# A mixture-of-experts kernel on one core: the first two tiles of each expert taken as a pair, with the weights held still and the tokens streamed

## The reference, cut to what matters

```python
xn = layernorm(x)                       # x: 2 x 1024 x 512, fp32; T = 2048 tokens
# routing: each token picks 6 of 32 experts
s = sigmoid(xf @ Wr.T + br)             # ... group-limited top-6 -> idx, weights w
gate = zeros(T, 32).at[arange(T)[:, None], idx].add(w)
# experts: W1 is 32 x 256 x 512, W2 is 32 x 512 x 256
for w1, w2, g in experts:
    acc += g[:, None] * (square(relu(xf @ w1.T)) @ w2.T)
shared = square(relu(xn @ Ws1.T)) @ Ws2.T
out = x + causal_attention(xn) + shared + acc
```

## Time and the profile before

| | |
|---|---|
| median of 3 runs | 1529.18 us (1529.16 to 1531.23) |
| the profiled execution, its own time | 1530.99 us |
| its span, first to last instruction | 1529.2 us |
| PE busy | 1516.1 us, 99% of the span |
| DVE busy | 1133.2 us, 74% |
| ACT busy | 838.2 us, 55% |
| POOL busy | 296.5 us, 19% |

### The profile page before, as it was taken

One profiled execution on the slowest core, in us unless ns is written; L12 is line 12 of the kernel. 1 busy time (PEld: TensorE's weight loads), 2 busy tenths in 40 slices (PEclk: granted clock), 3 DMA queues, 4 the chain that ended last, 5 costly groups with the idle time before them and its releaser, 6 DMA issues.

```text
span 1529.2 us, 31143 instructions
## 1 busy us (share of the span) xinstructions
PE 1516.1 (99%) x8548; PEld 1308.5 (86%) x8549; DVE 1133.2 (74%) x2586; ACT 838.2 (55%) x1753; POOL 296.5 (19%) x540
## 2 busy tenths in 40 slices
PE   9999999999999999999999999999999999999998
PEld 7887888989888978888888888888888888888886
DVE  7887566666666669949948958966975994994896
ACT  5565666766766635535535634544553563553553
POOL 0002443444444301012002002102102101200211
PEclk8999999999999999999999999999999999999999
DMA  7875677777776712102102103412211210210111
GB/s 277 322 283 188 199 240 235 242 236 226 237 257 200 240 41 70 43 21 75 42 20 75 42 34 103 164 62 82 68 35 36 74 41 21 75 34 27 56 42 55
DMA packets 64774, 184.34 MB, mean 121 GB/s; under 512 B 7136, under 2 KB 7264, under 8 KB 60000
## 3 DMA queue, kind: packets, MB, share of 16 engines
q1 hardware_dynamic: 39888, 112.56, 20.9%
q0 software_dynamic: 16640, 54.54, 13.0%
q10 hardware_dynamic: 8208, 16.78, 2.8%
HBM read 123.29 MB, written 60.56 MB: 120 GB/s over the span
## 4 chain that ended last, share of the span: by engine, by line
PE 97%; DVE 2%; DMA 1%; ACT 0%; issue 0%; SPq 0%; DVEq 0%; ACTq 0%
PE bank L663 8%; PE bank L665 8%; PE bank L994 8%; PE bank L664 8%; PE ps_s L663 7%; PE ps_s L665 7%; PE ps_s L664 7%; PE ps_s L981 5%; PE ps_s L983 4%; PE ps_s L982 4%; PE ps_s L861 4%; PE ps_s L865 3%; PE ps_s L884 3%; PE ps_s L862 3%; PE ps_s L885 3%; PE ps_s L888 3%
## 5 line engine op out<-in xcount | busy, mean ns | idle before, releaser
L1323 ACT ACTIVATE probs<-probs,negmax 128x128 f32<-128x128 f32 (+7 forms) x256 | 197.4, 773 | 122.6 <-DVE negmax L1737 121.9
L1331 ACT ACTIVATE pT_hi<-bank 128x512 fp32r<-128x512 f32 x288 | 164.4, 595 | 143.6 <-PE bank L994 117.6
L1348 DVE TENSOR_TENSOR pT_lo<-bank,pT_hi 128x512 fp32r<-128x512 f32 x288 | 189.6, 684 | 41.1 <-ACT pT_hi L1331 40.1
L1737 DVE CUSTOM_DVE_ANT_0 probs<-ps_s,causal 128x128 f32<-128x128 f32 (+7 forms) x256 | 189.3, 752 | 17.2 <-PE ps_s L983 15.7
L427 POOL TENSOR_TENSOR settled<-ident 128x1 f32<-128x1 f32 x192 | 46.0, 239 | 789.0 <-DVE acc L1766 779.0
L994 PE MATMUL bank<-ident,probs 128*128 128x128 f32 x1152 | 157.0, 272 | 0.0
L994 PEld LDWEIGHTS bank<-ident,probs 128*128 128x128 f32 x1152 | 136.9, 141 | 19.8
L663 PE MATMUL ps_s<-xT_hi,wa_hi 128*128 128x512 f32 x384 | 152.7, 398 | 0.0
L665 PE MATMUL ps_s<-xT_hi,wa_lo 128*128 128x512 f32 x384 | 151.0, 393 | 0.0
L664 PE MATMUL ps_s<-xT_lo,wa_hi 128*128 128x512 f32 x384 | 150.3, 391 | 0.0
L1746 DVE TENSOR_SCALAR probs<-probs,rnorm 128x128 f32<-128x128 f32 (+7 forms) x256 | 133.4, 521 | 9.1
(11 more groups left out here) (197 smaller groups left out, 3608.7 us busy)
## 6 DMA issues: line engine op xcount, KB each, us to landing
eraw<-we SPq DMA_DIRECT2D x37, 1024.0 KB, 7.4
expert_outputs<-ysb SPq DMA_DIRECT2D x111, 256.0 KB
araw<-wa SPq DMA_DIRECT2D x37, 512.0 KB, 3.8
expert_outputs<-comb ACTq DMA_DIRECT2D x1, 16384.0 KB, 44.2
normed_tokens<-xn SPq DMA_DIRECT2D x4, 1024.0 KB, 9.8
out<-acc SPq DMA_DIRECT2D x16, 256.0 KB, 2.6
acc<-x SPq DMA_DIRECT2D x2, 1024.0 KB, 13.7
turned_tokens<-xT_hi SPq DMA_DIRECT2D x2, 1024.0 KB, 6.3
```

The costliest lines, as they stand in the source:

```text
L1323: act.activation(pr, pr, ACT.Exp, bias=negmax[:, i % 2, a:a + 1], scale=-1.0, accum_out=rowsum[:, i % 2, a:a + 1]).then_inc(exp_ready, 1)
L1331: act.activation(pT_hi[:, blk % RING, :], ps_t[blk % 2][:, :], ACT.Copy).then_inc(pt_hi_ready, 1)
L1348: dve.tensor_tensor(out_, whole, upper.bitcast(F32), ALU.subtract).then_inc(signal, 1)
L1737: dve.tensor_tensor_reduce(halves(probs[:, i % 2, a, 0:keys]), ps_s[:, s:s + parts, 0:keys // parts], halves(causal[:, SQ - keys:]), -1.0, ...
```

## The change

The first two tiles of each expert become a pair. In their first layer the weights are stationary, 128 hidden units at a time, and the 256 tokens of both tiles stream past them (`hidden_pair`). The result comes out with hidden units on the partitions, so these two tiles need no `transpose_hidden`. The hidden values of the pair are made in two halves `m` on ACT and DVE. The output of the pair's first tile runs directly behind (`output_first`); that of the second is the `output_tile` of the next loop iteration. The remaining tiles run as before. Every expert is given at least three tiles (`LEAST`). The weight pieces 2 and 3 move from behind the tile loop into the pair.

```diff
-MAXT = MINT + 2 * E
+LEAST = 3
+MAXT = max(LEAST * (E - n) + min(n * TILES, (T * TOPK + (P - 1) * n) // P) for n in range(E + 1))
...
+        ps_x2 = banks[0][:, :]
+        ps_p = [bank[:, 0:2 * P] for bank in banks[1::2]]
+        ps_y2 = banks[2][:, :]
...
+            def hidden_pair(lo, s):
+                w_hi, w_lo = w1(hi_slot(s)), w1(lo_slot(s))
+                both = lambda x, k: x[:, k, :, :].rearrange("p t n -> p (t n)")
+                for m in range(KM):
+                    ms = slice(m * P, (m + 1) * P)
+                    if m == 0:
+                        pe.wait_ge(mx_hi, lo + 2)
+                    for k in range(KD):
+                        pe.matmul(ps_p[m], w_hi[:, k, ms], both(xgT_hi, k), start=(k == 0), stop=False)
+                        pe.matmul(ps_p[m], w_lo[:, k, ms], both(xgT_hi, k), start=False, stop=False)
+                    if m == 0:
+                        pe.wait_ge(mx_lo, lo + 2)
+                    for k in range(KD):
+                        mm = pe.matmul(ps_p[m], w_hi[:, k, ms], both(xgT_lo, k), start=False, stop=(k == KD - 1))
+                    mm.then_inc(mh_ready, 1)
+
+            def output_first(lo, s):
+                w_hi, w_lo = w2(hi_slot(s)), w2(lo_slot(s))
+                for m in range(KM):
+                    pe.wait_ge(mhhi_ready, past(lo + (m + 1)))
+                    pe.matmul(ps_y2, hT_hi[:, m, 0, :], w_hi[:, m, :], start=(m == 0), stop=False)
+                    pe.matmul(ps_y2, hT_hi[:, m, 0, :], w_lo[:, m, :], start=False, stop=False)
+                    pe.wait_ge(mhlo_ready, past(lo + (m + 1)))
+                    mm = pe.matmul(ps_y2, hT_lo[:, m, 0, :], w_hi[:, m, :], start=False, stop=(m == KM - 1))
+                mm.then_inc(my_ready, 1)
...
             def expert_tiles(e, s, lo, hi, es):
-                pe.wait_ge(ew_lo, (e + NSH) * WP + 2)
-                hidden_tile(lo, slot_of(s))
-                after = pair_bound(pe, e + 2)
+                turn_tokens(lo + 1, ps_x2)
                 if s:
                     output_tile(lo - 1, slot_of(s - 1))
                 else:
                     with pe.If(es > 0):
                         output_tile(lo - 1, slot_of(SLOTS - 1))
-                transpose_hidden(lo, (e + (NSH + 1)) * WP)
-                with pe.Fori(lo + 1, hi) as p:
+                after = pair_bound(pe, e + 2)
+                pe.wait_ge(ew_lo, (e + NSH) * WP + 2)
+                hidden_pair(lo, slot_of(s))
+                pe.sem_inc(mt_ready, 2)
+                turn_tokens(lo + 2, ps_x)
+                pe.wait_ge(ew_lo, (e + (NSH + 1)) * WP)
+                output_first(lo, slot_of(s))
+                with pe.Fori(lo + 2, hi) as p:
                     hidden_tile(p, slot_of(s))
                     output_tile(p - 1, slot_of(s))
                     transpose_hidden(p)
...
             def expert_uppers(e, s, lo, hi, es):
-                relu_hidden(lo)
-                upper_tokens(lo + 1)
+                upper_tokens(lo + 1, 1)
                 upper_weights(0, slot, arrived)
...
-                upper_hidden(lo)
                 after = pair_bound(act, e + 2)
                 upper_weights(1, slot, arrived)
-                with act.Fori(lo + 1, hi) as p:
+                relu_pair(lo, 0)
+                upper_pair(lo, 0)
+                upper_weights(2, slot, arrived)
+                relu_pair(lo, 1)
+                upper_pair(lo, 1)
+                upper_tokens(lo + 2)
+                copy_output(lo, ps_y2)
+                upper_weights(3, slot, arrived)
+                with act.Fori(lo + 2, hi) as p:
...
-                upper_weights(2, slot, arrived)
-                upper_weights(3, slot, arrived)
...
             def expert_lowers(e, s, lo, hi, es):
-                square_hidden(lo)
-                lower_tokens(lo + 1)
+                lower_tokens(lo + 1, 1)
                 lower_weights(e + 2, 0, slot)
-                lower_hidden(lo)
                 after = pair_bound(dve, e + 2)
                 lower_weights(e + 2, 1, slot)
-                with dve.Fori(lo + 1, hi) as p:
+                square_pair(lo, 0)
+                lower_pair(lo, 0)
+                lower_weights(e + 2, 2, slot)
+                square_pair(lo, 1)
+                lower_pair(lo, 1)
+                lower_tokens(lo + 2)
+                lower_weights(e + 2, 3, slot)
+                with dve.Fori(lo + 2, hi) as p:
...
-                chain(dve.tensor_scalar(pairs_f, pairs_f, 2.0, None, ALU.max))
+                chain(dve.tensor_scalar(pairs_f, pairs_f, float(LEAST), None, ALU.max))
...
+                        if isinstance(n, int) and n == 0 and unit == 0:
+                            dve.wait_ge(room_free, 1)
```

More of the change, by code:

```diff
@@ L219, in moe_attention_kernel @@
             xg = sb("xg", [P, XG, D], F32, room)
[L220 to L221 removed]
+            xgT_hi = sb("xgT_hi", [P, KD, 2, P], F32R, room)
+            xgT_lo = sb("xgT_lo", [P, KD, 2, P], F32R, room)
             ysb = sb("ysb", [P, YB, D], F32, room)
@@ L224, in moe_attention_kernel @@
             mhsq = sb("mhsq", [P, M], F32, room)
-            hT_hi = sb("hT_hi", [P, KM, P], F32R, room)
-            hT_lo = sb("hT_lo", [P, KM, P], F32R, room)
+            hT_hi = sb("hT_hi", [P, KM, 2, P], F32R, room)
+            hT_lo = sb("hT_lo", [P, KM, 2, P], F32R, room)
+            prelu = sb("prelu", [P, KM, 2 * P], F32, room)
+            phsq = sb("phsq", [P, KM, 2 * P], F32, room)
         with ExitStack() as room:
@@ L1242, in relu_hidden, with relu_pair, upper_pair, copy_output @@
                 act.activation(mrelu[:, :], ps_h, ACT.Relu).then_inc(mrelu_ready, 1)
+            def relu_pair(lo, m):
+                act.wait_ge(mh_ready, lo + (m + 1))
+                act.wait_ge(mhsq_ready, past(lo))
+                act.activation(prelu[:, m, :], ps_p[m], ACT.Relu).then_inc(mrelu_ready, 1)
+            def upper_pair(lo, m):
+                act.wait_ge(mrelu_ready, past(lo + (m + 1)))
+                act.activation(hT_hi[:, m, :, :].rearrange("p t n -> p (t n)"), prelu[:, m, :],
+                               ACT.Square).then_inc(mhhi_ready, 1)
             def upper_hidden(p):
                 act.wait_ge(mt_ready, p + 1)
-                act.activation(hT_hi[:, :, :], ps_g.rearrange("p (m n) -> p m n", m=KM), ACT.Copy).then_inc(mhhi_ready, 1)
-            def copy_output(p):
+                act.activation(hT_hi[:, :, 1, :], ps_g.rearrange("p (m n) -> p m n", m=KM), ACT.Copy).then_inc(mhhi_ready, 1)
+            def copy_output(p, bank=ps_y):
                 act.wait_ge(my_ready, past(p + 1))
                 act.wait_ge(y_free, p + 1)
-                act.activation(ysb[:, bass.ds(p % YB, 1), :].rearrange("p s d -> p (s d)"), ps_y,
+                act.activation(ysb[:, bass.ds(p % YB, 1), :].rearrange("p s d -> p (s d)"), bank,
                                ACT.Copy).then_inc(y_copied, 1)
@@ L1647, in _, with lower_tokens, square_pair, lower_pair @@
             dve.tensor_copy(tok_idx[:, 0:MAXT], ps_list).then_inc(list_ready, 1)
-            def lower_tokens(q):
+            def lower_tokens(q, second=0):
                 dve.wait_ge(mx_hi, q + 1)
-                subtract(xgT_lo[:, :, :], ps_x.rearrange("p (k n) -> p k n", k=KD), xgT_hi[:, :, :], mx_lo)
+                subtract(xgT_lo[:, :, second, :], (ps_x, ps_x2)[second].rearrange("p (k n) -> p k n", k=KD),
+                         xgT_hi[:, :, second, :], mx_lo)
+            def square_pair(lo, m):
+                dve.wait_ge(mrelu_ready, past(lo + (m + 1)))
+                dve.tensor_tensor(phsq[:, m, :], prelu[:, m, :], prelu[:, m, :], ALU.mult).then_inc(mhsq_ready, 1)
+            def lower_pair(lo, m):
+                dve.wait_ge(mhhi_ready, past(lo + (m + 1)))
+                dve.wait_ge(mhsq_ready, past(lo + (m + 1)))
+                subtract(hT_lo[:, m, :, :].rearrange("p t n -> p (t n)"), phsq[:, m, :],
+                         hT_hi[:, m, :, :].rearrange("p t n -> p (t n)"), mhlo_ready)
             def square_hidden(p):
@@ L1659, in lower_hidden @@
                 dve.wait_ge(mhhi_ready, past(p + 1))
-                subtract(hT_lo[:, :, :], ps_g.rearrange("p (m n) -> p m n", m=KM), hT_hi[:, :, :], mhlo_ready)
+                subtract(hT_lo[:, :, 1, :], ps_g.rearrange("p (m n) -> p m n", m=KM), hT_hi[:, :, 1, :], mhlo_ready)
             def lower_weights(e, c, slot):
```

50 lines of the change are left out of this document (24 added, 26 removed).

## The result

The changed kernel takes 1543.25 us (median of 4 runs, 1539.38 to 1546.65) against 1529.2: ratio 1.0102, 95% interval 1.0075 to 1.0129. It is slower by about 1%. The profiled execution's own time is 1546.65 us.

The account below looks back on a forecast made before the run. PE was taken to bound the kernel, so only its work and waits count. +0.41 us per expert times 31 gave +12.7, with +0.7 and +0.6 +14.0 us: 1545.0, less 1.8 for the median, 1543.2 us; range 1533 to 1554.

Parts of the forecast that it names:

- The sum: Per expert -0.43 - 0.20 + 0.71 + 0.33 = +0.41 us; times 31, +12.7; with +0.7 and +0.6, +14.0 us.
- The change of expert, +0.71: At the old expert's last output PE waits for ACT's `hT_hi`: latency 1.15 less 0.44 us cover, at 31 changes.
- Rival A: PE doesn't wait at the change of expert: 1521 us, or 1511 with no wait in the pair; chance 0.06.
- The pair, +0.33: In the pair, waits of 0.05 for `hT_hi` and 0.15 for `hT_lo`, plus 0.13 us loop entry, per expert.
- the entry of the tile loop: Behind the pair, entering the tile loop straight after a wait costs PE 0.13 us per expert.
- Rivals B and C: B: the pair costs PE nothing, 1533 us, chance 0.15. C: it costs twice as much, 1554 us, chance 0.12.
- The hidden transposes, -0.43: Four hidden transposes fewer on PE for each expert, 2 x 0.22 = 0.43 us saved.
- The old excess, -0.20: PE's old wait at the end of an expert's first tile, behind weight pieces 2 and 3, goes: 0.20 us per expert.
- Front and first expert, +0.7 and +0.6: Longer lists add 0.7 us to PE's mask products; in the first expert the third tile starts 0.6 us later.
- Rival D: Idle time at each change of expert lowers PE's clock: +53 us, 1597 us; chance 0.04.

Follow-up runs that it names:

- e2_fill: Changed kernel with three more 512-column products at each change of expert, between the next tokens' transposes and the last tile's output: 1552.71 us, ratio 1.0156.
- e6_merge: Changed kernel with the second tile's token transposes moved into the previous expert's last tile, under one branch tree with the first tile's: 1561.95 us, ratio 1.0210.
- e4_win: Changed kernel with the pair's first layer put ahead of the previous expert's last output and the second tile's tokens transposed earlier: 1520.16 us, ratio 0.9946.
- e5_win2: e4_win with the transposes of the next pair's two token tiles under one branch tree instead of two: 1509.59 us, ratio 0.9869.
- e11_behind: Kernel before with an added two-level branch tree on TensorE right behind each expert's first tile's hidden transposes: 1564.11 us, ratio 1.0211.
- e3_late2: Changed kernel with weight piece 2 moved from between the pair's halves to behind the split of the third tile's tokens: 1536.14 us, ratio 1.0045.
- e9_few: Kernel before with VectorE's subtraction of each expert's last weight piece cut to 8 columns: 1526.70 us, ratio 0.9974.
- e1_maxt: Kernel before with only its lists of tiles lengthened from 160 to 177, nothing of the pair: 1527.55 us, ratio 0.9984.
- e10_again: The changed kernel run once more, unchanged: 1543.38 us, ratio 1.0079.
- e7_soon: Kernel before with the third of four weight pieces put ahead of the loop over tiles instead of behind it: 1539.42 us, ratio 1.0078.

## Why the prediction was right

**The sum.** I forecast 1543.2 and measured 1543.25 and 1543.38. That is luck, closer than the terms: the experts cost 15.5 us instead of 13.3 (12.7 and the first expert's 0.6), and the attention stage gave back 2.6 that I didn't have. 15.5 - 2.6, with the 0.7 of the front, is 13.6. The mechanism is borne out all the same: per expert I had +0.41, and measured are 0.49 (15.5 less 0.3 for the first expert, over 31).

**The change of expert, +0.71.** Right in cause and size: 0.72 us in the timeline above, 0.73 on the mean. Three runs bear on the cause: added work goes into it (e2_fill), without the cover PE waits the full latency (e6_merge), and the wait vanishes when the pair covers it (e4_win and e5_win2). Rival A is refuted. What I didn't see is that a tree of branches now stands right behind the hidden transposes, whose operand PE may have to wait for. In the changed kernel the token transposes behind it begin up to 0.8 us late, but most of that lies beside ACT's latency: it adds 0.5 us over the five changes where it comes last. That the branches are the cause of this lateness is argued from e11_behind; no run takes them out of this place alone. In e4_win a second tree stands behind four token transposes (0.44 us) only, and there it shows: three-tile experts take 10.43 us on the mean, and 9.99 with the two trees joined (e5_win2), 10.9 us in the whole stage.

**The pair, +0.33.** Measured 0.36 us per expert around `output_first`. The sum is right, its parts are not. The wait for `hT_hi` was 0.06 us (0.05 forecast), that for `hT_lo` 0.29 (0.15 forecast), and the entry of the tile loop behind it, which I had at 0.13, cost nothing: from the load of L900 to the next tile's first product pass 0.34 us (318.96 to 319.30), the 0.1 and the 0.23 of any such product. It was DVE's piece ahead of `phsq` that made `hT_lo` late, as chained; what I had too short is what follows it, 0.10 us from the end of `phsq` to the start of `hT_lo` (318.38 to 318.48) and 0.06 from its end to the load. e3_late2 took 0.19 of the term away. Rivals B and C both fail. The Square takes 0.42 us where I took 0.40. By the Trainium skill (ScalarE: Activation LUTs, Rules for kernel authors), whose figure of 0.3 us per ACTIVATE is for a bias given as a pointer operand, it would be 0.51 us as an estimate; the row of 0.42 is below that.

**The hidden transposes, -0.43.** They fell from 222 to 94. e5_win2, with all waits gone, shows the term: a three-tile expert takes 9.99 us, three undisturbed tiles 3 x 3.475 = 10.43, so the four transposes that two tiles no longer have are worth 0.44.

**The old excess, -0.20.** Right as a whole: a three-tile expert took 10.65 us before, 0.22 over 10.43, and in e5_win2 nothing of it is left. The two terms together, 0.63, are what e5_win2 gained in the stage: 19.3 us, 0.62 for each of 31 experts. Its cause is shown in part only. e9_few removes the wait for `mhsq`, and with it 0.13 of the 0.16 us in the first tiles, though the stage as a whole gained just 0.07 per expert, because later tiles lengthened; some 0.04 us stood in the other tiles of an expert, where I had put nothing. The sum per expert with measured terms is -0.44 - 0.20 + 0.73 + 0.36 = +0.45, against 0.49 measured; 0.04 stays unassigned.

**Front and first expert, +0.7 and +0.6.** The longer lists cost too little to show in a total (e1_maxt), but 0.7 us between the mask products, as forecast, and the zero fill took 57.2 us where I had 56. In the first expert the third tile starts at 153.73 in place of 150.54, of which 2.9 us come from the later start of the stage (141.2 against 138.2); so +0.3. Four microseconds near its start had a granted clock of 0.57 again, as before.

**Rival D.** The granted clock was 1.00 from 154 to 550 us although PE lost 0.7 to 0.9 us at each of 31 changes of expert. The Trainium skill's warning (TensorE: Matmul & The Clock Gate, A second HAM failure mode) doesn't come true at these pauses. The rival's own premise, that the pause in the first expert brings the four slow microseconds and costs 1.7 us, isn't borne out by the changed kernel either. PE pauses there for 1.45 us in both traces of the changed kernel, but the clock fell in the first alone. Four microseconds at the same place in e10_again, whose stage begins 2.3 us earlier:

```profile
146.00:150.00 4.00, 3.74 (x24) 2.96 (x24) 2.63 (x5) 3.32 (x8) 0.57 (x2) 1.00 1.04 424
```

From the start of the stage to the third tile's first product pass 12.57 us with the slow stretch and 12.53 without it: in the changed kernel it costs next to nothing.

## What to carry to other kernels

A change that removes work may also remove what hid a latency: ask at each seam what stood between a producer and its reader. Where it is bare, put the next independent block there; the same pair, ahead of the last output instead of behind it and with its branches joined, turned +1.0% into -1.3%. Put branches behind a long run of products rather than right behind a semaphore that TensorE waits for.

## What was not expected of the hardware

- The same tree of branches on TensorE's queue costs nothing behind six products of 512 columns, and 0.99 us behind a wait that only two transposes follow.
- 68 bytes more in one on-chip allocation make the attention stage 2.6 us shorter (935.4 to 932.8 us), in every trace with the longer list. The first product of the projections takes a mean of 395 ns instead of 398 between 620 and 1400 us. Which address matters is open.
- The runs of one kernel differ by up to 11 us (1521 to 1532 for the one before). In the traces this lies ahead of the experts: mean granted clocks of 0.84 and 0.86 between 5 and 66 us in two traces of the same kernel, and first token transposes at 141.2 and 138.8 us; in e7_soon, 0.94 and 132.3 us.
